# The add that ends the rotary embedding of queries and keys: GpSimd does it for the first three groups of the first stage, VectorE for the other thirteen

## The reference

```
x = x + gnn0(layernorm(x), adj)
x = x + ffn0(layernorm(x))     # attention, then 8 experts, 2 per token
x = x + gnn1(layernorm(x), adj)
x = x + ffn1(layernorm(x))     # 6 small experts, 2 per token
```

```
q = q * cos + rotate_half(q) * sin
k = k * cos + rotate_half(k) * sin
scores = einsum('bhtd,bhsd->bhts', q, k) / sqrt(32)
```

## Time and profile before

| | |
|---|---|
| median of 3 runs | 855.65 us (854.5 to 856.88) |
| the profiled execution | 856.57 us |
| its span, first to last instruction | 854.5 us |
| PE busy in the span | 811.8 us (95%) |
| DVE | 697.2 us (82%) |
| ACT | 517.9 us (61%) |
| POOL | 426.2 us (50%) |

### The profile page before, as it was taken

One profiled execution on the slowest core, in us unless ns is written; L12 is line 12 of the kernel. 1 busy time (PEld: TensorE's weight loads), 2 busy tenths in 40 slices (PEclk: granted clock), 3 DMA queues, 4 the chain that ended last, 5 costly groups with the idle time before them and its releaser, 6 DMA issues.

```text
span 854.5 us, 21578 instructions
## 1 busy us (share of the span) xinstructions
PE 811.8 (95%) x6292; PEld 628.6 (74%) x6293; DVE 697.2 (82%) x2699; ACT 517.9 (61%) x1072; POOL 426.2 (50%) x410
## 2 busy tenths in 40 slices
PE   6988999999888899999999999899999999999998
PEld 6666777767547899999999999566666666666663
DVE  4899898989767698877777888888888888888863
ACT  3667778787546466556565654556555556655654
POOL 4248888888777200930100052566665566666300
PEclk9999999999999999999999999999999999999999
DMA  9603311131115766676666662333333344443322
GB/s 270 177 18 90 99 51 53 46 115 42 44 41 171 196 190 172 173 195 167 173 169 167 173 181 73 112 122 125 122 124 119 118 144 152 140 131 121 108 88 99
DMA packets 104711, 108.25 MB, mean 127 GB/s; under 512 B 27278, under 2 KB 88672, under 8 KB 102464
## 3 DMA queue, kind: packets, MB, share of 16 engines
q1 hardware_dynamic: 94096, 88.52, 35.8%
q0 software_dynamic: 8880, 18.19, 7.1%
q10 hardware_dynamic: 1664, 0.66, 0.3%
HBM read 82.07 MB, written 25.26 MB: 126 GB/s over the span
## 4 chain that ended last, share of the span: by engine, by line
PE 62%; issue 3%; POOL 1%; DVE 1%; DMA 1%; SPq 0%; ACT 0%; POOLq 0%; DVEq 0%; ACTq 0%
PE banks L2062 17%; PE banks L2102 10%; PE banks L2228 9%; PE banks L2220 9%; PE banks L2196 7%; PE banks L2077 2%; PE banks L2123 2%; PE banks L2134 1%; PE banks L2151 1%; PE banks L2242 1%; PE banks L2163 1%; POOL expert_rows L1345 1%; PE banks L2172 1%; PE banks L2143 1%; DMA slots_out<-ys 0%
## 5 line engine op out<-in xcount | busy, mean ns | idle before, releaser
L1345 POOL DMA_INDIRECT expert_rows<-slots_out,slot_c x128 | 141.8, 1108 | 75.9 <-DVE ys L1601 43.9
L326 POOL DMA_INDIRECT slots_in<-flat,slot_now x115 | 120.7, 1050 | 35.7 <-issue 31.2
L2062 PE MATMUL banks<-xT_hi,w_hi 128*128 128x256 f32 (+1 forms) x426 | 126.8, 298 | 0.4 <-DVE w_lo L1620 0.4
L2062 PE MATMUL banks<-xT_hi,w_lo 128*128 128x256 f32 (+1 forms) x426 | 120.5, 283 | 0.0
L2062 PE MATMUL banks<-xT_lo,w_hi 128*128 128x256 f32 (+1 forms) x426 | 120.2, 282 | 0.0
L2102 PE MATMUL banks<-w_sb,prod 128*128 (+1 forms) x852 | 107.7, 276 | 2.7 <-DVE ys L1601 2.7
L2102 PEld LDWEIGHTS banks<-w_sb,prod 128*128 128x128 f32 (+1 forms) x852 | 101.8, 192 | 3.3 <-issue 3.1
L2062 PEld LDWEIGHTS banks<-xT_hi,w_hi 128*128 128x128 f32 (+1 forms) x426 | 76.0, 178 | 0.6 <-issue 0.6
L2062 PEld LDWEIGHTS banks<-xT_lo,w_hi 128*128 128x128 f32 (+1 forms) x426 | 76.4, 179 | 0.0
L2062 PEld LDWEIGHTS banks<-xT_hi,w_lo 128*128 128x128 f32 (+1 forms) x426 | 76.1, 179 | 0.0
L1419 ACT ACTIVATE w_hi<-w_raw 128x684 fp32r<-128x684 f32 x71 | 54.9, 773 | 26.6 <-PE banks L2062 26.2
(11 more groups left out here) (305 smaller groups left out, 2117.7 us busy)
## 6 DMA issues: line engine op xcount, KB each, us to landing
f_all<-gates_dram SPq DMA_DIRECT2D x16, 1536.0 KB, 6.1
w_raw<-in_w SPq DMA_DIRECT2D x71, 342.0 KB, 3.4
xs<-slots_in SPq DMA_DIRECT2D x71, 128.0 KB, 2.6
slots_out<-ys SPq DMA_DIRECT2D x71, 128.0 KB, 3.2
base_all<-in_x SPq DMA_DIRECT2D x16, 256.0 KB, 4.1
out<-ob SPq DMA_DIRECT2D x16, 256.0 KB
slots_in<-zrow SPq DMA_DIRECT2D x20, 128.0 KB
adjt<-in_adj_t SPq DMA_DIRECT2D x32, 64.0 KB, 2.4
```

Source lines behind the costliest of these rows:

```text
L326: G.indirect_dma_start(out=slots_in, out_offset=bass.IndirectOffsetOnAxis(ap=slot_now0[g % 2][:, n:n + 1], axis=0), in_=flat[g % 2][:, n / ...
L1345: G.indirect_dma_start(out=rows[p][:, n, :], out_offset=None, in_=slots_out[0:filled(g) * R, :], in_offset=bass.IndirectOffsetOnAxis(ap=sl ...
L2062: last = T.matmul(banks[bank][0:m, half * R:(half + 1) * R], ww[:, par, n * HIDP + c * P:n * HIDP + c * P + m], xx[:, par, :], start=q == ...
```

## The change

For groups 0, 1 and 2 (`EARLY = 3`) the add of `qk_cos` and `qk_sin` into `qk_rot` leaves DVE's list and is issued by POOL, between `ln_pow(new)` and the first scatters of its iteration, with the same waits. From group 3 on DVE does it where it did. `qkr` gets a semaphore of its own, since two engines now count it up, and DVE's step waits for the add of the group before.

```diff
+            EARLY = 3
-            in_order(..., "qks qkc qkr vl", "x1 st1",
+            in_order(..., "qks qkc vl", "qkr", "x1 st1",
@@ POOL
+                    def qkr(g):
+                        if g is not None and g < EARLY:
+                            pool.wait_ge(at["qkc"], upto("qkc", g + 1))
+                            pool.wait_ge(at["qks"], upto("qks", g + 1))
+                            if exists(g - 1):
+                                pool.wait_ge(at["scores"], upto("scores", g))
+                            G.tensor_tensor(qk_rot[:, :, :], qk_cos[:, :, :], qk_sin[:, :, :], ALU.add).then_inc(at["qkr"], 1)
@@ POOL's body
                         ln_pow(new)
+                        qkr(g[3])
                         scatter(2, g[6])
@@ DVE
                     def qkr(g):
-                        if g is not None:
+                        if g is not None and g >= EARLY:
+                            dve.wait_ge(at["qkr"], upto("qkr", g))
```

More of the change, by code:

```diff
@@ L207, in build @@
             at, step_of = {}, {}
-            in_order("ln_st ln_mv ln_var ln_nm", "mv1 var1 nmr inv ratio", "max sub", "lg top topi topf oh sel rk ohr", "slotf slot dtop", "qks qkc qkr vl", "x1 st1",
+            in_order("ln_st ln_mv ln_var ln_nm", "mv1 var1 nmr inv ratio", "max sub", "lg top topi topf oh sel rk ohr", "slotf slot dtop", "qks qkc vl", "qkr", "x1 st1",
                      "pqs pks pq", *"ln_pow xn gnnT tT gnn rstd1 hp hT hTc pk v vd scores exp prT prTc y rden yn yT yTc wo f2 ssq ssv rms flat ssum rank deg".split())
```

## The result

| | before | changed |
|---|---|---|
| median of 20 runs each | 856.82 us | 860.30 us |
| lowest to highest | 854.26 to 861.12 | 858.81 to 866.15 |
| ratio, 95% interval | | 1.0038 (1.0023 to 1.0054) |
| span of the profiled execution | 854.5 us | 857.8 us |

The changed kernel is slower by 0.38%, 3.3 to 3.5 us, where 2.0 us was forecast. The interval is clear of no change, and the cost is above the 2.6 us up to which the forecast's own case (chance 0.55) reached; costs over 2.6 us had 0.28. The time lies on the upper end of the range, 860.3, with nothing to spare. The forecast was added to a median of three runs, 855.65; over 20 runs the kernel before has 856.82, which accounts for 1.17 of the 2.65 us between the forecast 857.65 and the measured 860.30.

The account below looks back on a forecast made before the run. The date of POOL's first scatter was taken to set the first stage's end: 1.3 us from group 0 plus 1.0 from group 2, less 0.7 back, taken as 2.0, so 855.65 + 2.0 = 857.65 us; range 854.8 to 860.3.

Parts of the forecast that it names:

- the forecast's own case: The end of the first stage comes 1.3 to 2.6 us late; chance 0.55.
- costs over 2.6 us: Case that POOL's add holds DVE at `sel`, or that the add takes longer; chance 0.28.
- What bounds the stage: First stage: POOL runs a fixed-length list from its first scatter at 59.53 us; that date sets the end.
- The add on POOL: One 128 x 1024 add takes 2.40 us on POOL, against 1.22 on DVE.
- Group 0: The add ends 1.29 us later, ahead of the mask matmuls; PE is 1.3 us late.
- Group 1: PE reaches the mask matmuls after the add; DVE's saved 1.22 us becomes waiting: neither gain nor loss.
- the sum: First scatter 2.3 us late (1.3 + 1.0), 0.7 back; stage end 1.6 to 2.3 late, 2.0 taken.
- Group 2: `rms(0)` stands behind the add on POOL and ends 1.22 us later; first scatter 1.03 us later.
- the rival: At group 2, POOL's add holds DVE's `sel`: first scatter 2.5 us late, 3.3 in all; chance 0.28 including a longer add.
- the 0.7 us that were to come back: The scatter at 70.12, held by DVE's group 3 add, would be held only 0.1 us, returning 0.7.
- the held `sel`: DVE's `sel` waits for POOL's group 2 add: 3.3 us slower, 859.0; chance 0.28 including a longer add.

Follow-up runs that it names:

- before with the cut load: The kernel before, its one adjacency load cut into eight loads over iterations 8 to 15: 856.79 us, ratio 0.9992.
- group 1 alone: The kernel before with only group 1's add moved to POOL: 859.91 us, ratio 1.0028.
- group 2 alone: The kernel before with only group 2's add moved to POOL: 858.14 us, ratio 1.0020.
- group 2 behind `sel`: The kernel before with only group 2's add on POOL, waiting there for DVE's `sel` of the same iteration: 858.62 us, ratio 1.0015.
- `rms` first: The changed kernel with `rms` of group 0 ahead of group 2's add in POOL's list: 861.15 us, ratio 1.0031.
- the changed kernel again: The changed kernel measured once more without an edit: 861.06 us, ratio 1.0039.
- the two changed ones with the cut load: The changed kernel with the adjacency load in eight parts, 860.46 us; the same plus ten zero matmuls ahead of group 0's scores, 860.06 us.
- group 0 alone: The kernel before with only group 0's add moved to POOL: 860.24 us, ratio 1.0029.
- the kernel with all adds on POOL: The changed kernel with the adds of all sixteen groups on POOL (`EARLY = 16`): 902.69 us, ratio 1.0507.

## Why the prediction was right, point by point

**What bounds the stage: right, with a slack at its end.** In nine profiles (before, before with the cut load, group 1 and group 2 alone, group 2 behind `sel`, `rms` first, the changed kernel again, and the two changed ones with the cut load) the second stage's first transposes come 201.0 to 202.1 us after the first scatter. A loss at the first scatter is a loss at the end of the stage. In the two profiles with a stop of some 3 us (the changed kernel and group 0 alone) they come at 203.8 and 204.2. What the prediction missed is POOL's wait of 1.21 us for DVE at 234.46, a little behind the stretch that it read: by then POOL's list doesn't end the stage alone.

**The add on POOL: right.** 2.35 us, forecast 2.40. The estimate by the Trainium skill, 2.25, lay 0.1 us off on the other side.

**Group 0: right.** 1.17 us, forecast 1.29. By group 2's cosine product 0.98 of it was left, which the sum had not allowed for. What it left out besides is that PE's clock fell to half behind the 1.45 us of idleness in three of the six profiled executions that had it, for 1.2 to 1.4 us more; no execution without the wait did.

**Group 1: right.** 0.1 us, DVE's time turned into a wait.

**Group 2: right in size, wrong about DVE.** The add costs the first scatter 1.03 us in the changed kernel and 1.09 alone, forecast 1.03. The prediction let DVE pass and be held 0.3 us at `ratio`. The held step was `ssv`, one step ahead of the `sel` of the rival (both are of group 0; the prediction wrote group 1 for `sel`), and counted from group 2's cosine product DVE was 1.0 us later for it (`x1` at 2.57 us instead of 1.54, `slot` done at 4.92 instead of 3.89). The rival's mechanism was thus there, and `slot` ended 0.06 us behind `flat`; but `rms` was as late, so the rival's 2.5 us at the first scatter were 2.0. The Trainium skill says in SBUF — State Buffer, section "Who interferes with whom", that when GpSimd and a VectorE instruction in a two-port mode, which a `tensor_scalar` can enter, want the shared ports, whoever issues first has them for its whole instruction and the other stands still. That `ssv` ran in such a mode no row shows; its 2.33 us instead of 0.16, from 0.04 us behind the add's start to 0.02 behind its end, agree with it.

**The failed step: the 0.7 us that were to come back.** The sum had the scatter that was held 1.82 us run free, since POOL would be 2.3 us late and DVE only 1.3 to 1.5. Counted from group 0's cosine product, POOL was 2.0 us late and DVE, held at `ssv`, 2.1 (its add at 73.14, before at 69.88, the product 1.14 later), so the two met as before and the hold was 1.95 us. In its place the runs show 2.0 us at the first scatter, 0.1 more at that scatter, and 0.07 us in each of some eleven later iterations; then the last iterations give back about 1.5 us, most of it because POOL doesn't wait for `ssv` there. In the changed kernel again, the profile without a long stop and without a fall of the clock, the sum of this is 1.4 us at the last `rms` and at SP's first load of the second stage, and 2.2 at the first transposes, whose data took 3.0 us to come instead of 2.2. That the forecast of 2.0 us is so near is partly luck: 0.3 us too much at the first scatter, a return from a place where none came, and another, unforeseen, at the stage's end.

**The rest, up to 3.5 us, is only in part explained.** Some executions have the fall of the clock behind group 0's wait (three of six profiled ones with it, of which one was of the kernel with all adds on POOL; over all executions that would be some 0.7 us by an estimate of half of 1.2 to 1.4) and PE's stop behind the adjacency load, with the clock at half behind the long ones (2.0 and 2.4 us more at the transposes than in before). The stop alone doesn't make the difference, as with the cut load 3.7 us stayed. How often the clock falls in unprofiled executions stays open, and so do the 2.5 us of group 1 alone, of which its trace shows nearly nothing. A rival that no run tests is that the changed program as such, with its other code and semaphores, costs something ahead of or behind the first stage: group 0's cosine product, ahead of every moved add, ended at 30.4 to 31.1 us in the four profiles with the old semaphore and at 30.2 to 31.6 in the ten with the new one, 0.4 later in the mean. So the time came into the range by the range's width, which the prediction had for the held `sel` and the spread of a median, and at its very edge.

## What to carry to other kernels

An idle engine isn't a free one: POOL was mostly idle ahead of its first scatter, and still the add delayed PE by its extra length and the `rms` queued behind it. Before moving a step, find the one date that the slow phase hangs on, and ask of each engine what stands behind the moved step in its list. When two engines share SBUF ports, also look at which small steps with their inputs in SBUF start while the moved instruction runs: the two that did here lasted until it ended, whether they started 0.04 us behind its start (`ssv`) or 1.6 (`ratio`). And read the waits to the very end of the phase: a wait just behind the stretch that was read (here at 234 us) says that the limit changes there.

## What the runs showed of the hardware

- A VectorE `tensor_scalar` of 128 x 4 took 2.33 us when it started 0.04 us behind a GpSimd add of 128 x 1024, and 0.16 us otherwise. Two-input steps were held in the same way (`ratio` 1.51 us in the kernel with `rms` first and 0.73 with group 2's add behind `sel`, instead of 0.15), also when they started 0.9 to 1.7 us behind the add's start. A 128 x 512 add with an input from PSUM that ran beside group 0's add took its usual 0.69 us.
- An indirect DMA issue on GpSimd that starts while VectorE adds two SBUF inputs took 1.55 to 1.95 us instead of 0.97; moving the add 0.35 us earlier took 0.25 us off each. The Trainium skill (SBUF — State Buffer, section "Who interferes with whom") infers that a tensor_tensor leaves descriptor generation alone; these rows show a hold of the whole issue instruction, whichever part of it waits.
- TensorE stopped for 0.97 to 3.17 us within 64 small matmuls in five of nine profiles with the adjacency load in one piece and the stage at its usual pace, each time behind an instruction queue's packet that arrived while the DMA share was over 1.0; in the other four of the nine a packet came during the load too, or at its end, and PE didn't stop. With the load cut into eight the stops in four profiles were 0, 0, 0.39 and 0.89 us, the last with a DMA share of at most 0.2. Behind the two stops of some 3 us the granted clock was at half for 3.4 us; behind those of 1.53 us and less it stayed at 1.00.
